# Fetching three gathered rows per stationary column instead of two, with the table as four byte fields, in a four-layer graph network on one core

## The reference

```python
# block 0: GIN             agg = segment_sum(x[src], dst); two dense layers, batch norm
# block 1: GIN             agg = segment_sum(x[src], dst); three dense layers (64-256-256-64)
# block 2: three message layers of
m   = relu(concat([h[src], h[dst], edge_features]) @ msg_W1[l] + msg_b1[l]) @ msg_W2[l] + msg_b2[l]
h   = gru_cell(segment_sum(m, dst), h)
# block 3: two attention layers of
h   = x @ W
e   = leaky_relu(alpha_s[src] + alpha_d[dst]);  w = exp(e - segment_max(e, dst)[dst])
out = segment_sum(w / z[dst] * h[src], dst) + b
```

## Time and profile before

| | |
|---|---|
| median of 3 runs | 2670.47 us (2667.33 to 2694.43) |
| profiled execution: its time, its span | 2680.27 us, 2678.5 us |
| busy: TensorE, DVE, ACT, POOL | 2166.2, 1901.9, 839.4, 1813.7 us |
| mean granted TensorE clock | 0.889 of full speed |
| DMA | 635.94 MB, 237 GB/s mean |

### The profile page before, as it was taken

The page is one execution under the profiler, slowest core; times in us unless marked ns, Lnnn a source line. Parts: engine busy times, 40 slices in busy tenths (PEclk is TensorE's granted clock), DMA queues, the critical chain, the costliest instruction groups (busy, mean ns, idle before and its releaser), DMA issues.

```text
span 2678.5 us, 59128 instructions
## 1 busy us (share of the span) xinstructions
PE 2166.2 (81%) x21135; PEld 1868.1 (70%) x21135; DVE 1901.9 (71%) x6907; ACT 839.4 (31%) x2462; POOL 1813.7 (68%) x1766
## 2 busy tenths in 40 slices
PE   6799279996998898688888688988679995599971
PEld 6788149996577786367776367776359995499971
DVE  9999745887367777477777667777546777457776
ACT  1122131121321221322212222212345666346663
POOL 6877737777477666577667677667556667677773
PEclk9899659999899998699999889999769998599995
DMA  8999818996178888378888368888246776368861
GB/s 285 322 345 391 243 29 291 377 352 244 48 246 283 286 303 278 86 234 275 299 277 300 108 229 271 305 278 300 84 105 212 266 252 201 94 223 258 260 219 41
DMA packets 299539, 635.94 MB, mean 237 GB/s; under 512 B 106923, under 2 KB 130677, under 8 KB 275780
## 3 DMA queue, kind: packets, MB, share of 16 engines
q1 hardware_dynamic: 223584, 545.67, 57.5%
q0 software_dynamic: 56160, 56.36, 9.8%
q10 hardware_dynamic: 19588, 31.50, 3.3%
HBM read 450.51 MB, written 182.82 MB: 236 GB/s over the span
## 4 chain that ended last, share of the span: by engine, by line
DVE 31%; PE 27%; ACT 14%; DMA 10%; issue 9%; POOL 6%; ACTq 1%; SPq 1%; DVEq 0%; POOLq 0%
PE ps L1844 16%; ACT big L843 7%; DVE ringG L1278 7%; PE ps L1802 4%; DMA edge_side<-q_at_start 4%; ACT ringG L872 4%; DVE ringG L1398 3%; DVE edge_side L1278 3%; PE ps L1872 3%; POOL ringG L755 3%; DMA ef_mix<-edge_side 2%; DVE ringG L1258 2%; POOL nodes L755 2%; PE ps L1811 2%; DVE ringG L1250 2%
## 5 line engine op out<-in xcount | busy, mean ns | idle before, releaser
L1844 PE MATMUL ps<-big 128*128 128x192 f16 (+1 forms) x17929 | 1626.8, 251 | 26.0 <-DMA big<-kept 20.0
L755 POOL DMA_INDIRECT ringG<-tab,src_i x1234 | 1255.3, 1017 | 540.6 <-issue 354.3
L1844 PEld LDWEIGHTS ps<-big 128*128 128x128 fp8e5 x17929 | 1541.8, 99 | 68.2 <-issue 39.1
L1278 DVE SCALAR_TENSOR_TENSOR ringG<-ringG,same 128x64 f32<-128x64 f32 x2075 | 577.6, 278 | 26.1 <-DMA ringG<-tab,src_i 0.9
L1278 DVE SCALAR_TENSOR_TENSOR edge_side<-edge_side,same 128x64 f32<-128x64 f32 x1245 | 345.2, 277 | 109.8 <-DMA edge_side<-q_at_start 105.4
L843 ACT ACTIVATE big<-ps 128x384 int32<-128x384 f32 (+3 forms) x670 | 257.0, 483 | 354.2 <-PE ps L1844 354.2
L861 ACT ACTIVATE ringG<-ringG 128x512 f32<-128x512 f32 x156 | 98.2, 630 | 716.2 <-DVE ringG L1358 712.2
L755 POOL DMA_INDIRECT ringG<-in_x,src_i x216 | 247.2, 1144 | 78.2 <-issue 63.1
L1398 DVE SCALAR_TENSOR_TENSOR ringG<-ringG,expo 128x65 f32<-128x65 f32 x830 | 236.6, 285 | 64.1 <-DVE ringG L1398 2.3
L1872 PE MATMUL ps<-edge_side,ident 128*128 128x512 f32 x312 | 179.8, 660 | 121.0 <-DVE edge_side L1278 105.8
L872 ACT ACTIVATE ringG<-ringG,expo 128x65 f32<-128x65 f32 x832 | 210.5, 335 | 0.0
(11 more groups left out here) (284 smaller groups left out, 1820.7 us busy)
## 6 DMA issues: line engine op xcount, KB each, us to landing
big<-kept SPq DMA_DIRECT2D x156, 1152.0 KB
sums<-ringG SPq DMA_DIRECT2D x260, 256.0 KB
big<-kept SPq DMA_DIRECT2D x78, 720.0 KB
big<-kept SPq DMA_DIRECT2D x78, 576.0 KB
edge_side<-ef_mix SPq DMA_DIRECT2D x156, 256.0 KB, 3.2
edge_side<-q_at_start SPq DMA_DIRECT2D x156, 256.0 KB
kept<-big SPq DMA_DIRECT2D x26, 1152.0 KB, 9.0
sums_w<-ringG SPq DMA_DIRECT2D x104, 264.0 KB
```

What stands on the lines that cost most here:

```text
L755: return pool.indirect_dma_start(out=out_ap, out_offset=None, in_=table, in_offset=bass.IndirectOffsetOnAxis(ap=index, axis=0))
L1278: return v.scalar_tensor_tensor(now, before if u == 0 else source[:, (u - 1) * D:u * D], same[:, c:c + 1], now, ALU.mult, ALU.add)
L1844: mm = pe.matmul(ps[:, b, 0:2 * n] if wide else ps[:, b, to:to + n], hot[t][:, unit.us[u] * P:(unit.us[u] + 1) * P], opener[:, 0:2 * n] if ...
```

## The change

Three edges share a stationary column, at 2^-15, 2^-7 and 2^1, and the table streams as its own bytes: four float16 columns of one byte each per feature, 256 moving columns a matmul (264 in the attention passes). A product sum, times 32768, is an integer whose bytes 0, 1 and 2 are the same byte of three edges' rows. ACT makes one integer copy per chunk of two units and then three byte copies (`e::4`) straight into the slots of `ringG`; DVE only repairs equal sources, with three `copy_predicated` per chunk. A chunk serves groups 0 and 1 (one unit each), group 2, or group 3 (two units each). Hot columns: `FULL = (1, 1, 2, 2)`, 18 hot and 14 cold, now in pass 0 too; message passes (0, 1, 2, 2), 15 hot and 17 cold (8, 5, 2, 2 by group); last trip (0, 0, 2, 2), 12 and 20. The planes of codes go from 7 to 13, for stationary tiles of 768 instead of 1152 columns. The products of the message passes move one group back, and `evict` stands ahead of `clip`.

```diff
-FULL = (2, 2, 2, 3)
+FULL = (1, 1, 2, 2)
+EACH = 3
+COPIES = [(1, 2), (0, 1), (0, 2)]
+GROUPS_OF = [range(0, 2), range(2, 3), range(3, 4)]
...
-PLANES = [range(0, 1), range(1, 3), range(3, 5), range(5, 7)]
+PLANES = [range(0, 2), range(2, 6), range(6, 10), range(10, 13)]
...
-UNITS = [(FEW, FEW, FEW_LAST), (HOT, HOT, LAST)] + [(FEW, FEW_NEAR, FEW_LAST)] * NLAYER + [(HOT, NEAR, LAST), (HOT, HOT, LAST)]
+UNITS = [(HOT, HOT, LAST), (HOT, HOT, LAST)] + [(FEW, FEW, LAST)] * NLAYER + [(HOT, HOT, LAST), (HOT, HOT, LAST)]
...
-            def evict(k, i, banks=None):
...
-                for b in banks:
-                    n = min(2, unit.u - 2 * b)
-                    act.wait_ge(bank_done, BANKS_BEFORE[k] + way.before(i) + b + 1)
-                    of = ps[:, b, 0:n * size].rearrange("p (u k d) -> p u k d", u=n, k=3)
-                    for x, scale in enumerate((TO_INT, TO_HIGH)):
-                        ins = nc.scalar.activation(got[:, x, :, 2 * b:2 * b + n].rearrange("p k u d -> p u k d"), of,
-                                                   ACT.Copy, scale=scale)
-                    ins.then_inc(evicted, 1)
+            def evict(k, i):
...
+                for x, m in enumerate(unit.chunks):
+                    us, count = unit.of_chunk(m), CHUNKS_BEFORE[k] + way.before(i) + x + 1
+                    act.wait_ge(chunk_done, count)
+                    act.wait_ge(placed, CHUNKS_BEFORE[k] + way.before(i))
...
+                    nc.scalar.activation(got[:, us[0]:us[-1] + 1], of, ACT.Copy, scale=TO_INT).then_inc(evicted, 1)
+                    js = unit.groups_of(m)
+                    for j in js:
+                        act.wait_ge(slot_open[slot_of(k, g + j)], 16 * stores_before(k, g + j))
+                    if g + js[-1] >= RING:
+                        act.wait_ge(summed, k * NG + g + js[-1] - RING + 2)
+                    act.wait_ge(evicted, OPEN + count)
+                    s0, h = slot_of(k, g + js[0]), FULL[js[0]]
+                    for e in range(EACH):
+                        at = unit.start(js[0], e) * n
+                        ins = nc.scalar.activation(
+                            rows[:, s0:s0 + len(js), at:at + h * n].rearrange("p j (h n) -> p (j h) n", h=h) if len(js) == 1 else
+                            rows[:, s0:s0 + len(js), at:at + n],
+                            bytes_of[:, us[0]:us[-1] + 1, e::4], ACT.Copy)
+                    ins.then_inc(placed, 1)
...
                         elif 2 <= k < 5:
+                            if wanted_next(k, g):
+                                evict(k, (g + 1) // GROUPS)
                             clip(k - 2, g)
...
-            def take_piece(k, i, s):
...
+            def twin_piece(k, i, m, x):
...
+                if x == 0:
+                    v.wait_ge(placed, CHUNKS_BEFORE[k] + way.before(i) + unit.chunks.index(m) + 1)
+                else:
+                    v.wait_ge(vchain, taken[0])
...
+            def fix_between(k, g, u):
+
+                if u in (3, 5, 7):
+                    m = chunk_of_group(k, g)
+                    if m is not None:
+                        twin_piece(k, g // GROUPS, m, (u - 3) // 2)
...
-                split, n = split_of(way), 3 * way.width
+                split, n = split_of(way), 4 * way.width
...
-                                pe.wait_ge(evicted, at(way.banks, OPEN + BANKS_BEFORE[k] - way.banks + b + 1))
...
+                            if t == 0 and not first:
+                                pe.wait_ge(evicted, at(CHUNKS, OPEN + CHUNKS_BEFORE[k] - CHUNKS + m + 1))
...
                 for q in range(len(TILES)):
                     fetch_piece(k, 1, *trip_of(1), q, way.most)
-                    single(q + 2)
+                    single(q + 1)
```

More of the change, by code:

```diff
@@ L159, in __init__, with of_chunk, groups_of @@
         self.hot, self.u = hot, sum(hot)
-        self.banks = -(-self.u // 2)
         self.first = next(j for j in range(GROUPS) if hot[j])
-        self.us = [at for j in range(GROUPS) for at in range(self.tile(j), self.tile(j) + hot[j])]
-    def tile(self, j):
-        return sum(FULL[:j + 1]) - self.hot[j]
+        self.us = range(UMAX - self.u, UMAX)
+        self.chunks = [m for m in range(CHUNKS) if any(u in self.us for u in (2 * m, 2 * m + 1))]
+    def of_chunk(self, m):
+        return [u for u in (2 * m, 2 * m + 1) if u in self.us]
+    def groups_of(self, m):
+        return [j for j in GROUPS_OF[m] if self.hot[j]]
     def cold(self, j):
-        return COLS - 2 * self.hot[j]
+        return COLS - EACH * self.hot[j]
     def start(self, j, which):
-        return COLS - self.hot[j] - (0 if which else FULL[j])
+        return COLS - (EACH - which) * FULL[j]
     def cold_columns(self, j):
[L174 to L189, removed]
+        return list(range(self.cold(j)))
     def columns(self, which):
@@ L891, in act_pass @@
                     load_features(1)
-                evict(k, 0)
+                if PASSES[k].unit(0).first == 0:
+                    evict(k, 0)
                 for i in range(TRIPS):
@@ L1109, in split_chunk @@
             def split_chunk(c):
-                way, t = PASSES[2], slice(tiles(c).start, tiles(c).stop)
-                return split_rows(split_of(way)[:, t], pq.bitcast(U32)[:, t, 0:D], way.width)
+                t = slice(tiles(c).start, tiles(c).stop)
+                return v.tensor_copy(split_of(PASSES[2])[:, t], pq.bitcast(U8)[:, t, 0:4 * D])
             def make_codes():
-                number, plane, bit0, bit1, of = (stage[m] for m in range(5))
+                number, plane, odd, keep, of = (stage[m] for m in range(5))
@@ L1831, in fetch_piece @@
                 settle()
[L1832 to L1834 removed]
+                by_chunk = q in (0, len(TILES) - 1)
+                for ms in ([[m] for m in unit.chunks] if by_chunk else [unit.chunks]):
                     for t in TILES[q]:
[L1836 to L1848 removed]
```

359 lines of the change are left out of this document (161 added, 198 removed).

## The result

The changed kernel takes **2497.54 us** (median of 4 runs, 2495.7 to 2499.22), the kernel before 2671.39 us beside it: ratio 0.933, 95% interval 0.928 to 0.939. The forecast was 2525 with a range of 2455 to 2650. The profiled execution took 2498.38 us with a span of 2496.6, where the steps of the forecast gave 2533.

A forecast was written before the change was run, and what follows sets the result against it. Bounds: TensorE nearly full in passes 1, 5, 6, less so in message passes; DVE in pass 0; POOL close behind everywhere. Changes of -36, -11, -60, -25, -15 make -147 us: 2533 profiled, 2523 at the median; forecast 2525, range 2455 to 2650.

The forecast's parts named there:

- Attention passes: Passes 5 and 6: trips of 18.9 us through ACT and DVE; -25 us in pass 5, -15 in pass 6.
- Message passes: Passes 2 to 4: POOL bounds at 22.5 us a trip; each pass 314 us, -20, three times -60.
- the product costs nothing: Message passes: the edge product coming a group later costs nothing, as its trip's rows are needed a group later too.
- the 18: Message passes: 18 us kept of the 43 us for the tail and what stalls remain, in each pass.
- Pass 1: Pass 1: 188 gathers x 1.333 = 251 us and 8 more, a gain of 11 us.
- first case of rival (b): POOL: fewer wide DVE steps and lighter DMA bring every gather to 0.95 us, some 55 us let through: 2470; chance 0.11.
- sum of rival (b): POOL's run shrinks by 188 x (0.19 + 0.08) + 672 x 0.07 = 98 us.
- second case of rival (b): POOL: nine DVE copies each hold a gather up, 0.9 us more in the 65 trips POOL bounds: 2585; chance 0.11.
- DVE's copies: DVE: nine copy_predicated a trip replace four, at 0.225 us each, adding 1.1 us.
- Pass 0: Pass 0: 188 gathers x 1.44 = 271 us and 24 for start and tail, 295: -36 us.
- Rival (a): ACT: byte copies cost twice (1.06 us), +14 us in all: about 2685, no change; chance 0.12.
- Rival (c): Passes 1, 5 and 6: new waits put TensorE at its lower clock, slower than before, 2737 at f = 0.4; chance 0.06.

The follow-up runs named there:

- heavy_feed: The changed kernel with half as many bytes again copied from the kept tiles to spare memory with each feed in passes 1 to 6: 11.3 us more.
- no_twins: The changed kernel with all nine copy_predicated a trip left out (rows of repeated edges stay wrong): 36.3 us less.
- copies_twice: The changed kernel with each of ACT's byte copies made twice, the extra one into a spare buffer: 2.0% slower than the kernel before.
- one_copy_more: The changed kernel with one of the three byte copies of each chunk made a second time into a spare buffer: +62 us.

## Why the prediction was right, and where it was not

**TensorE** was right: 109.1 ns for the 109 worked out from the slope between 192 and 384 columns.

**ACT** was right on the copy (0.527 for 0.53). In message passes it was slack, as forecast.

**Attention passes.** The forecast put the loop through ACT and DVE at 18.9 us, TensorE's at 18.3 and POOL's at 18.2. The trips took 18.4 to 18.5 (from one `evict` to the next). With TensorE relieved they stayed, and with DVE relieved they stayed; with ACT's stretch 0.7 us shorter they were 17.7. So the loop of the forecast was there and half a us shorter, and TensorE's stood right beside it.

**Message passes.** POOL bounds (22.4 us for 22.5), and the product costs nothing: both shown. The size was off by 32 us in three passes. In pass 2 the forecast has 296 us of gathers and 18 for the tail and what stalls remain; measured are 223 x 1.312 = 292.6 and 13.3 of tail. Over the three passes 15 us come from the pace of the gathers (1.298 to 1.312 us for 1.321), 14 from the 18, since no stall remained, and 3 from the windows, which take the passes before 1 us too short.

**Pass 1** gained 22.8 for 11. The forecast multiplied 188 gathers by the old 1.333 us; they came every 1.277. This is the first case of rival (b). In passes 1, 5 and 6 a gather is 0.05 to 0.08 us shorter, for which `heavy_feed` rules the traffic out. What was removed beside it are DVE's wide steps of the take; before, in pass 5, the 13 gathers that the step at line 1244 overlapped took 1.38 us in the mean, the others 0.97. That points to them, but no run put them back alone. The sum of rival (b) also left out passes 5 and 6, where the gathers shrank as well.

**The second case of rival (b)** was true at the same time, smaller: `no_twins` shows that nine copies cost the message passes 24 us. The two cases are not alternatives, as I had them, but two terms of opposite sign, and the first was larger.

**DVE's copies** are 231.1 / 798 = 0.29 us each, not 0.225. The earlier trace rows gave 292 ns for one; the forecast divided the busy time of the group, in which instructions that overlap count once.

**Pass 0** is the step that failed: 16.4 us for 36. The forecast was 188 x 1.44 = 271 and 24 for the start and the tail. The gathers with their issue took less, 188 x 1.40 = 264 us; but POOL waited 39 us and the tail was 13.4, so the 24 were more than 50. The three waits of 17.23, 8.45 and 5.21 are 30.9 us of it: a slot opens when its group is summed and stored, whatever a gather costs. The kernel before had 32 gathers in its eight slots, where 28 fill them now, and then waited 10.60 us:

```profile
60.83 1.33 POOL L755 DMA_INDIRECT ringG<-in_x,src_i  x1 [10.60 <-DMA sums<-ringG]
```

The slot opens 1.4 us later now, since DVE starts its first running sum at 50.93 instead of 46.73 us. The forecast had 5 us more for preparing codes and 4 less for the table. It had nothing for the wait of DVE's first match for the codes, before and after:

```profile
21.58 1.55 DVE L1159 TENSOR_SCALAR nodes<-nodes,node_f 128x1152 uint8<-128x1152 uint8 x2 [1.18 <-DMA big<-codes]
```

```profile
27.32 1.68 DVE L1160 TENSOR_SCALAR nodes<-nodes,node_f 128x768 uint8<-128x768 uint8 x3 [6.49 <-DMA big<-codes]
```

In all, TensorE's first opener came 5.8 us later (31.3 for 25.5), the eleven trips behind it took 18.1 less and the rest 4.1 less. In mid-pass the trips were 20.5 us before and are 19.0 to 19.3: 1.4 less and not 2.8, for DVE saved less than that. By form, 60 to 250 us, one piece of eight tiles costs it the first three of these; the last stands in a piece of five:

```profile
L1171 DVE TENSOR_TENSOR big<-big,nodes 128x768 uint32<-128x768 uint32 x19 | 18.2, 960 | 0.0
...
L1181 DVE TENSOR_SCALAR big<-big 128x768 uint32<-128x768 uint32 x19 | 11.8, 620 | 0.0
L1180 DVE TENSOR_SCALAR big<-big 128x768 uint32<-128x768 uint32 x19 | 10.6, 559 | 0.0
...
L1181 DVE TENSOR_SCALAR big<-big 128x576 uint32<-128x576 uint32 x9 | 6.7, 746 | 0.0
```

The forecast's 0.54 ns a word and 0.14 us an instruction give 0.55 us for 768 words and 0.45 for 576; one of the two shifts meets that, the other does not. The copies took 9 x 0.29 us. Behind DVE, TensorE's trip of 19.1 us, POOL and the DMA engines (0.93 to 1.03) stand close, so each relieved alone gave 0 to 5 us: four tiles less 0, no copies 5, fewer codes another 5.

**Rival (a)** is out by the duration of the copies. **Rival (c)** did not come, but the mechanism exists: `copies_twice` lost 2.6 us a trip to the clock and ended slower than the kernel before. It was nearer than 0.06 said: half a microsecond more per chunk already lowered the clock in some trips of `one_copy_more`.

## What to carry to other kernels

Where an engine with a queue of its own (here POOL's gathers) stands close behind the bound, price a change by that queue's pace and count, and look for what in its neighbours stretches its instructions: their length is not a constant of the kernel. Where two loops are equally long, relieving either shows nothing; shorten what they share (here ACT's stretch), and read the trips by themselves, since a pass can gain at its start alone. A pass whose slots fill before its consumer starts does not gain from a faster producer until the consumer starts. Once the bound has moved, ask which split between the two ways of fetching fits now: here one more stationary column in each trip of the message passes, for three gathers, was worth 60 us that the change itself had left.

## What the runs showed that I had not expected

In the message passes, POOL gathers into which a DVE copy of 0.30 us fell 0.10 to 0.20 us behind their start took 1.23 us in the mean instead of 0.96; in pass 1 they took 0.94. TensorE's granted clock fell to 0.85 of full speed over a pass whose trips had waits of 2.69 and 1.44 us, and to 0.91 in some trips, not in others, with waits of 1.64 and 0.40. Byte copies with a source step of four cost ACT no more than its integer copies of as many columns (0.52 to 0.53 us back to back for 512; 0.58 to 0.60 for one integer copy).
